# Factorised pair scores with a small tower: 31 units a chunk, TensorE's order written out, later fields transposed in the product ring

## The reference, cut to what matters

```python
e = jnp.stack([tbl_0[ids[:, 0]], ..., tbl_31[ids[:, 31]]], axis=1)      # 512 x 32 x 64
p, q = e[:, ids_x, :], e[:, ids_y, :]                                   # 496 pairs
z = jnp.einsum('bpj,bpj->bp', jnp.einsum('bpi,pij->bpj', p, w), q)      # 512 x 496
h = jnp.concatenate([z, dense_ctx], axis=1)                             # 512 x 512
h = jnp.maximum(h @ W_top1 + b_top1, 0.0)
h = jnp.maximum(h @ W_top2 + b_top2, 0.0)
y = h @ W_top3
```

## Time and profile before

| what | value |
|---|---|
| time, median of 3 runs | 263.83 us (263.15 to 263.94) |
| span of the profiled execution, first to last instruction | 217.7 us |
| around the span (median less span) | 46.1 us |
| PE busy | 196.1 us, 90% |
| DVE busy | 174.1 us, 80% |
| ACT busy | 150.4 us, 69% |
| POOL busy | 150.2 us, 69% |
| mean granted TensorE clock | 0.992 of full speed |

### The profile page before, as it was taken

How to read it: one execution, slowest core, us unless ns; L and a number is a source line. 1 busy time by engine, 2 the same in 40 slices (tenths; PEclk the granted TensorE clock), 3 DMA queues, 4 the chain that set the end, 5 groups by cost and what they waited for, 6 DMA issues and landing times.

```text
span 217.7 us, 6053 instructions
## 1 busy us (share of the span) xinstructions
PE 196.1 (90%) x2072; PEld 131.6 (60%) x2072; DVE 174.1 (80%) x159; ACT 150.4 (69%) x1146; POOL 150.2 (69%) x186
## 2 busy tenths in 40 slices
PE   0029899699999989999999999999999999999985
PEld 0007553575758549556786556865677755767874
DVE  0003789679999999999998999979989989897911
ACT  2010268299799957998199896599959978999201
POOL 4777777777777777777777777777788718777300
PEclk9999999969999999999999999999999999999999
DMA  5666656667111111111111111111110000000000
GB/s 190 252 222 223 230 205 223 218 215 229 30 25 29 35 24 29 29 24 32 25 27 32 27 24 34 25 29 30 29 27 6 2 3 0 2 5 0 3 0 3
DMA packets 6432, 15.21 MB, mean 70 GB/s; under 512 B 2689, under 2 KB 2945, under 8 KB 5250
## 3 DMA queue, kind: packets, MB, share of 16 engines
q1 hardware_dynamic: 2306, 10.62, 13.7%
q0 software_dynamic: 4096, 4.20, 9.3%
HBM read 14.82 MB, written 0.00 MB: 68 GB/s over the span
## 4 chain that ended last, share of the span: by engine, by line
PE 79%; POOL 12%; issue 4%; DMA 3%; ACT 1%; DVE 0%; DVEq 0%
PE pu L485 25%; PE pu L477 24%; PE pz L498 13%; POOL emb L284 12%; PE pt L505 6%; PE pt L452 4%; PE pt L517 3%; DMA emb<-in_tbl,idx 3%; PE pu L505 1%; PE pt L527 1%; DMA idx<-in_ids 1%; PE pt L463 1%; PE pu L517 0%; ACT eT L303 0%; DVE zT L421 0%
## 5 line engine op out<-in xcount | busy, mean ns | idle before, releaser
L284 POOL DMA_INDIRECT emb<-in_tbl,idx x128 | 120.9, 945 | 41.1 <-issue 30.2
L312 ACT ACTIVATE turned<-turned 128x64 f32<-128x64 f32 x544 | 130.2, 245 | 1.5 <-DVE turned L389 1.5
L312 ACT ACTIVATION_READ_ACCUMULATOR turned<-turned 128x1 f32 x544 | 104.1, 191 | 0.0
L389 DVE TENSOR_TENSOR turned<-pu,emb 128x1024 f32<-128x1024 f32 x64 | 75.9, 1215 | 8.1 <-PE pu L477 7.8
L407 DVE TENSOR_TENSOR prod<-pu,eT 128x1024 f32<-128x1024 f32 x48 | 57.1, 1216 | 23.4 <-PE pu L485 23.3
L485 PEld LDWEIGHTS pu<-eT,ws 64*128 64x128 f32 x1024 | 64.9, 198 | 11.8 <-issue 10.4
L485 PE MATMUL pu<-eT,ws 64*128 64x128 f32 x1024 | 69.2, 287 | 0.0
L477 PE MATMUL pu<-ws,eT 64*128 64x512 f32 x256 | 65.5, 612 | 0.0
L303 ACT COPY eT<-pt 128x128 f32<-128x128 f32 (+1 forms) x28 | 11.2, 398 | 41.6 <-PE pt L452 41.6
L270 POOL TENSOR_TENSOR turned<-turned 128x512 f32<-128x512 f32 (+4 forms) x45 | 27.3, 607 | 11.4 <-DVE turned L389 8.4
L477 PEld LDWEIGHTS pu<-ws,eT 64*128 64x128 f32 x256 | 21.1, 186 | 16.7 <-issue 15.1
(11 more groups left out here) (24 smaller groups left out, 25.4 us busy)
## 6 DMA issues: line engine op xcount, KB each, us to landing
ws<-in_w SPq DMA_DIRECT2D x8, 1024.0 KB, 5.0
emb<-in_tbl,idx POOLq DMA_INDIRECT x128, 2.4
w1s<-in_w SPq DMA_DIRECT2D x1, 1024.0 KB
zT<-in_dense SPq DMA_DIRECT2D x1, 512.0 KB, 4.1
w2s<-in_w SPq DMA_DIRECT2D x1, 512.0 KB
idx<-in_ids SPq DMA_DIRECT2D x1, 64.0 KB, 1.8
identity<-in_ident SPq DMA_DIRECT2D x1, 64.0 KB, 1.8
w3s<-in_w SPq DMA_DIRECT2D x1, 1.0 KB
```

What stands on the lines that cost most here:

```text
L284: nc.gpsimd.indirect_dma_start(out=emb[:, c % EC, x, :], out_offset=None, in_=tables[x], in_offset=bass.IndirectOffsetOnAxis(ap=idx[:, c, ...
L312: i = nc.scalar.activation(t, t, ACT.Copy, accum_out=zB[:, b // NT % 2, b % NT * 16 + v:b % NT * 16 + v + 1])
L389: nc.vector.tensor_tensor(turned[:, b % RB, :, :].rearrange("p (x f) i -> p x (f i)", x=2), u.rearrange("p x s i -> p x (s i)"), e, ALU.mu ...
```

## The change

**Units.** 31 units of 16 blocks hold the 496 pairs without empty blocks. The four "b" units are gone; three new units a chunk, "c0" to "c2", hold what they held, each over all 32 fields. "c" units are turned ones (samples on the partitions), but made of eight matmuls of 128 moving columns of weights, since their blocks need different fields as stationary operand. A chunk has 13 "four" units and 3 "c" units turned (16 in all, as before) and 15 units summed (16 before). The dense rows stand in the rows that no pair takes.

**Ring.** The fields of the third and fourth chunk are transposed into buffers of `pu`, eight pairs (a whole buffer) at a time in the third and four in the fourth; such a group takes a turn of the ring, and ACT copies it with one instruction. The first two chunks go through `pt` as before.

**Order.** The order of the units in each chunk, and all of PE's other work (field groups `x`, partition sums `s`, tower steps), is written out in `UNIT_ORDER` and `PLAN`; layer 1 is one step instead of two. `ROWS` is new: ACT sums 38 turned units instead of 34, DVE 16 instead of 21, POOL 10 instead of 9.

**Tail.** In the last chunk each block of layer 1 has its own signal, layer 2 runs over the inputs in the outer loop, and layer 3 takes its two halves as they come.

```diff
     UNITS += [("four", _k, 4 * _m) for _k in range(4 * _j, 4 * _j + 4) for _m in range(_j)]
-    UNITS += [("a", 4 * _j + 3, 4 * _j), ("b", 4 * _j + 3, 4 * _j)]
+    UNITS += [("a", 4 * _j + 3, 4 * _j)]
+UNITS += [(_c, KP - 1, 0) for _c in C_X]
...
+C_X = {"c0": ((0, 3), (5, 3), 1), "c1": ((3, 1), (2, 5), 1), "c2": ((1, 0), (6, 3), 4)}
...
+UNIT_ORDER = [[0, 1, 2, 3, 4, 6, 7, 5, 8, 9, 11, 14, 12, 10, 13, 16, 17, 15, 20, 18, 19, 23, 22, 21, 30, 29, 25, 26,
+               28, 24, 27],
...
-XN = [1, 4, 4, 4]
+X_SIZES = [[1, 1, 1, 1, 1, 1, 1, 1, 1, 1, 1, 1, 1, 1, 1, 1],
+           [4, 4, 4, 4],
+           [8, 8],
+           [4, 4, 4, 4]]
+X_RING = (False, False, True, True)
...
+PLAN = [(-1, 'x', 0), (-1, 'x', 1), (-1, 'x', 2), (-1, 'x', 3), (-1, 'x', 4), (1, 'x', 5), (1, 's', 0), (2, 'x', 6),
+        (2, 's', 1), (3, 'x', 7), (3, 'x', 8), (7, 'x', 9), (7, 'x', 10), (9, 's', 2), (9, 'x', 11), (14, 'x', 12),
...
+            def copy_ring_x(g):
+                c, k, n = GROUPS[g]
+                act.wait_ge(xr_ready, RING_X.index(g) + 1)
+                if c >= EC:
+
+                    act.wait_ge(mult_done, (c - EC + 1) * NU)
+                nc.scalar.copy(eT[:, c % EC, k:k + n, :].rearrange("p s b -> p (s b)"),
+                               pu[:, TURN["x", g] % UR, :, :, :].rearrange("p x s b -> p (x s b)")[:, 0:n * P]).then_inc(xr_read, 1)
...
+            def ring_free(what, v):
+                n = TURN[what, v]
+                if n >= UR:
+                    kind, before = RING[n - UR]
+                    if kind == "u":
+                        pe.wait_ge(mult_done, before + 1)
+                    else:
+                        pe.wait_ge(xr_read, RING_X.index(before) + 1)
+
+            def transpose_ring_x(g):
+                c, k, n = GROUPS[g]
+                ring_free("x", g)
+                for i in range(n):
+                    pe.wait_ge(s_emb[c * KP + k + i], 16 * 2)
+                    mm = nc.tensor.transpose(pu[:, TURN["x", g] % UR, i // 4, i % 4, :],
+                                             emb[:, c % EC, 2 * (k + i):2 * (k + i) + 2, :].rearrange("p f e -> p (f e)"), identity[:])
+                mm.then_inc(xr_ready, 1)
...
+                if UNITS[u][0] in C_X:
+                    for slot in range(4):
+                        for bank in range(2):
+                            x = slot_of(u, bank, slot, 0)[0]
+                            rows = slice(EMB * (x % 2), EMB * (x % 2 + 1))
+                            i = nc.tensor.matmul(pu[:, unit_slot(t), bank, slot, :], eT[rows, c % EC, x // 2, :], ws[rows, u, slot, :],
+                                                 start=True, stop=True)
+                    i.then_inc(u_ready, 1)
+                    return
...
+            for i in L1_LAST:
+                if i < N1 // 2:
+                    pe.wait_ge(h1_act, i + 1)
+                else:
+                    pe.wait_ge(h1_dve, i - N1 // 2 + 1)
+                for n in range(N2):
+                    mm = nc.tensor.matmul(l2_out(last, n), w2s[:, i, n * P:(n + 1) * P], h1[:, i, :],
+                                          start=(i == L1_LAST[0]), stop=(i == L1_LAST[-1]))
```

More of the change, by code:

```diff
@@ L48 @@
 Z_ORDER = [z for z in range(ZCH) if z >= ZA] + list(range(ZA))
-assert NU == 32 and NT == 16 and all(UNITS[u][0] == "four" for u in TURNED)
+assert NU == 31 and NT == 16 and all(UNITS[u][0] != "a" for u in TURNED) and not any(UNITS[u][0] in C_X for u in SUMMED)
 assert ZCH * P == FIELDS * (FIELDS - 1) // 2 + DENSE
-TURN_AT = [TURNED, [5, 6, 7, 8, 9, 14, 16, 17, 18, 19, 20, 21, 22, 23, 26, 29], [2, 6, 7, 8, 9, 10, 14, 16, 17, 22, 23, 24, 26, 27, 28, 30], [0, 5, 9, 10, 11, 13, 14, 15, 18, 19, 20, 22, 23, 24, 25, 26]]
@@ L53 @@
[L53 to L64, removed]
@@ L115 @@
 WU = 4
+NW = -(-NU // WU)
 W_AT_ONCE = 2
-XN = [1, 4, 4, 4]
-GROUPS = [(c, k, XN[c]) for c in range(BCH) for k in range(0, KP, XN[c])]
-NG = len(GROUPS)
[L127 to L134, removed]
@@ new lines, with l1_place @@
+assert [v[0] for v in PLAN] == sorted(v[0] for v in PLAN)
+assert [v[2] for v in PLAN if v[1] == "x"] == list(range(NG))
+SUMS = [v[2] for v in PLAN if v[1] == "s"]
+assert SUMS == list(range(len(SUMS))) and all(v[0] > STEP_A[v[2]] for v in PLAN if v[1] == "s")
+USERS = [v[1:] for v in PLAN if v[1] != "s" and not (v[1] == "x" and in_ring(v[2]))]
+PLACE = {v: i for i, v in enumerate(USERS)}
+def l1_place(c, i):
+    return next(PLACE[part, c] for part in L1_PARTS if i in L1_PARTS[part] and (part, c) in PLACE)
@@ L155, in dlrm_tower, with unit_slot @@
+RING = [v for t in range(-1, NS) for v in [("u", t)] * (t >= 0) + [v for v in TURNS[t] if v[0] == "x" and in_ring(v[1])]]
+TURN = {v: n for n, v in enumerate(RING)}
+NR = len(RING)
+PT_X = [g for what, g in USERS if what == "x"]
+RING_X = [g for what, g in RING if what == "x"]
+assert all(v[0] == "u" for v in RING[NR - UR:])
+def unit_slot(t):
+    return TURN["u", t] % UR
+Z_OUT = [33, 65, 92]
 def dlrm_tower(nc, tables, ids, w, dense, w1, b1, w2, b2, w3, ident, out):
@@ L219, in cols, with x_copied @@
             return slice(c * P, (c + 1) * P)
-        def by_vector(c, n, of):
-            return c == last and n >= of // 2
+        def x_copied(engine, c, k):
+            if not X_RING[c]:
+                engine.wait_ge(pt_read, PLACE["x", GROUP_OF[c, k]] + 1)
+            else:
+                engine.wait_ge(xr_read, RING_X.index(GROUP_OF[c, k]) + 1)
+        L1_LAST = (0, 2, 1, 3)
         def l1_out(c, n):
@@ L325, in layer1 @@
                     act.wait_ge(h2_ready, c)
-                for n in range(2 * half, 2 * half + 2):
-                    i = nc.scalar.activation(h1[:, n, :], l1_out(c, n), ACT.Relu, bias=b1s[:, n:n + 1])
+                for n in ns:
+                    i = nc.scalar.activation(h1[:, n, :], pt[:, n, :], ACT.Relu, bias=b1s[:, n:n + 1])
                 i.then_inc(pt_read, 1)
```

299 lines of the change are left out of this document (165 added, 134 removed), and 11 rows, old and new, of the table PLAN.

## The result

| | time, us (median; lowest to highest) |
|---|---|
| kernel before | 263.88 (263.15 to 264.08) |
| changed kernel | 267.90 (266.14 to 268.95) |
| ratio, 95% interval | 1.016 (1.013 to 1.019) |

What follows compares the result with a forecast made beforehand. PE was taken to bound the kernel from some 42 us to z3. z3 3.6 us sooner, +0.7 +0.5 +0.5 for waits, seams and ring, -0.3 tail: -2.2, so 215.5 plus 46.1 around it is 261.6 us; range 259.7 to 264.4.

Steps and rivals of the forecast that it cites:

- The 46.1 us around it, taken as unchanged.: Time outside the profiled execution, added to the forecast 215.5 us to give 261.6 us.
- x19 starts sooner: Second chunk's last field group on PE: forecast to start at 84.2 us, against 87.77 in the profile before.
- the tail is shorter: After z3, starting the first half of the last chunk's final steps one matmul sooner saves 0.3 us (0 to 0.5).
- PE is there before 84.05 and waits for the last field.: At x19, PE arrives by 81.9 or 83.6 us, before the second chunk's last gather lands at 84.05.
- x19 later than 85 us: Sign of being wrong: the first chunk would cost more than the prediction thought.
- 117.6 + 0.7 + 0.5 + 0.5 - 0.3: From x19 to z3: PE work 117.6, layer 2 wait 0.7, seams 0.5, ring 0.5, transposes before the wait -0.3 us.
- A "c" unit at 0.89: PE's price in us for a new eight-matmul unit, taken from a summed unit; 1.78 if matmuls don't overlap.
- the copy of 1024 columns at 1.0 us: ACT's copy of a ring buffer's field group, 128x1024: 1.0 us by slope, 0.58 as lower end.
- The seams of "c1" and "c2", taken as 0.5: Nine seams after x19 where two same-half matmuls meet: 0 to 0.11 us each; the skill's rule says full 0.11.
- The rivals: All cover holds, 259.9 us (0.18); clock falls, 263.3 (0.13); ACT bounds, 264.8 (0.13); slow "c" units, 269.6 (0.03).
- The slower side: Rival: ACT becomes the bound between x19's copy and the copies behind step 92, giving 264.8 us; chance 0.13.
- the clock fall behind x19: Rival: PE waits 2 us at x18 or x19 and its clock drops, +1.7 us, 263.3 us; chance 0.13.

Runs made afterwards that it cites:

- e1: The kernel before, unchanged, run and profiled once more: 260.5 us.
- e2: The changed kernel, unchanged, run and profiled once more: 266.5 us, ratio 1.024 to the kernel before.
- e7: Changed kernel with early first-chunk row sums b = 0 and 2 moved from ACT to DVE, b = 3 and 4 to later steps: ratio 1.012 to the kernel before.
- e11: Kernel before with 32 gathers instead of 128: only fields 0 to 7 of each chunk gathered, the others filled once by plain transfers: 218.6 us.
- e12: Changed kernel with 32 gathers instead of 128, other fields filled once by plain transfers: 219.5 us.
- e13: Changed kernel with 32 gathers and early first-chunk row sums b = 0 and 2 moved from ACT to DVE, b = 3 and 4 later: 217.2 us.
- e4: Changed kernel with only the first 1 MB of the 8 MB of unit weights loaded, every unit reading one of four blocks: 271.5 us.
- e3: Kernel before with only the first 1 MB of the 8 MB of unit weights loaded, every unit reading one of four blocks: 264.3 us.
- e17: Kernel before without gathers: SP brings every field's rows by 128 plain transfers with the same semaphore counts: 214.0 us.

## Why the prediction was wrong, step by step

*"The 46.1 us around it, taken as unchanged."* Wrong, and the root. They lie inside the span of the timed executions: 216.7 with 32 gathers, 256.3 with 128. Had I asked why a span of 217.7 stands beside a time of 263.8, the profile would have been known as one of another kind.

The sum had three terms against the kernel before: x19 starts sooner, the work from x19 to z3 is longer, the tail is shorter. From TensorE's timelines, us:

| | x19 starts | x19 to z3 | z3 to the end |
|---|---|---|---|
| before, profile ahead of the prediction | 87.7 | 117.3 | 12.6 |
| changed, forecast | 84.2 | 119.0 | 12.3 |
| before, timed (e1) | 116.5 | 127.1 | 12.6 |
| changed, timed (e2) | 118.4 | 133.8 | 12.0 |
| changed, rows to DVE (e7) | 115.6 | 135.0 | 12.0 |
| before, 32 gathers (e11) | 85.4 | 118.7 | 12.6 |
| changed, 32 gathers (e12) | 85.4 | 120.3 | 12.0 |

In the timed executions x19 came 1.9 us later instead of 3.6 sooner, and the stretch behind it grew by 6.6 us instead of 1.7. Both steps failed, about equally.

*"PE is there before 84.05 and waits for the last field."* This is the first step of the sum that failed. The first chunk's loss was costed at nothing because x19 would wait for its gather anyway. In the timed executions the 64th gather is issued at 94.2 us (e1) and 100.2 (e2), and PE comes to x19 only at 116.5 and 118.4. The rows are GpSimd's 64th gather and TensorE's x19 and z3, of e1 and then of e2:

```profile
94.15 0.94 POOL L284 DMA_INDIRECT emb<-in_tbl,idx  x1 [0.30 <-issue]
...
116.51 0.66 PE L452 MATMUL pt<-identity,emb 128*128 128x128 f32 x4
...
243.64 0.44 PE L463 MATMUL pt<-identity,zB 128*128 128x128 f32 x2
```
```profile
100.21 0.94 POOL L340 DMA_INDIRECT emb<-in_tbl,idx  x1 [0.30 <-issue]
...
118.37 0.65 PE L544 MATMUL pt<-identity,emb 128*128 128x128 f32 x4
...
252.13 0.44 PE L555 MATMUL pt<-identity,zB 128*128 128x128 f32 x2
```

Landing takes 2.4 us, so no wait for a gather stood there to hide anything, and the sign of being wrong, x19 later than 85 us, came. What made PE late is in part ACT's row sums ahead of x9's copy, which I had seen, but not counted: without them x19 comes 2.8 us sooner (e7 against e2) and, with fast hand-offs, 2.3 (83.1 in e13 against 85.4). With fast hand-offs the term is 0.0 and not -3.6: e11 and e12 both start x19 at 85.4, where I had PE ready at 83.6.

*PE's work from x19 to z3 and the waits in it.* 117.6 + 0.7 + 0.5 + 0.5 - 0.3 was forecast, about 1.7 more than before. With fast hand-offs it is 1.6 more: right in total, though not in its parts. Within it PE waited 0.4 us for ACT at layer 2 (0.7 forecast) and 1.8 once for DVE, which the sum didn't have. In the timed executions it is 6.6 more (e2 against e1), and this is the second step that failed: PE is idle for 7.8 us against 4.1, mostly for DVE's multiplications, and its groups take 126.0 against 123.1. VectorE's waits from x19 to z3, of e1, e2 and e12 (us in total, times, longest):

```profile
DVE turned L389 <- PE pu L477: 7.4, 9, 1.6
DVE prod L407 <- PE pu L485: 6.8, 7, 1.7
```
```profile
DVE prod L483 <- PE pu L584: 8.2, 7, 2.2
DVE turned L474 <- PE pu L569: 7.2, 2, 6.6
...
DVE prod L483 <- PE pu L576: 5.1, 5, 1.6
```
```profile
DVE turned L483 <- PE pu L578: 7.2, 2, 6.6
```

The longest, 6.6 us, stands at step 67, where sums, layer 1, x21 and layer 2 follow one another on PE and no unit is ready for DVE. But it stands in e12 as well, where the stretch is only 1.6 us longer: it belongs to the order and is not what slow hand-offs add. That a whole field group in a ring buffer leaves fewer units to cover a slow hand-off is my reading of the third chunk (+3.2 us timed, +0.1 with 32 gathers); no run undid the ring alone, so which part of the new order costs these us stays open.

*Sizes.* A "c" unit at 0.89 was right (chain of the changed kernel: start us, us), and so was the copy of 1024 columns at 1.0 us; the tail's 0.3 was 0.6 (12.6 against 12.0):

```profile
137.93 0.89 PE pu L569 x16
```
```profile
L367 ACT COPY eT<-pu 128x1024 f32<-128x1024 f32 x2 | 2.0, 1020 | 0.6 <-PE pu L535 0.6
```

The seams of "c1" and "c2", taken as 0.5, cost nothing. From the last matmul of one unit to the first of the next, start to start, e12's trace has 0.105 us at seven of the nine seams, as between two summed units, and 0.42 at the two behind a turned unit, as between a turned and a summed one. So the trace doesn't agree with the rule by which each would cost 0.11. In e12's chain "c0" and "c1" take 0.20 + 2 x 0.89, and two summed units behind "c1" 1.79:

```profile
92.62 1.99 PE pu L578 x32
94.61 1.79 PE pu L593 x32
```

*The rivals.* None came. The slower side was argued with ACT behind x19; there PE waited for ACT for only 0.5 us (e2), and ACT was late before it. (The 264.8 had no sum behind it: +2.1 on 261.6 is 263.7, no slower than before.) Nor did the clock fall behind x19: from x19 to z3 it was granted at 1.00 in e1 and e2. It did fall in the stalls, but there it weighs little: two executions of e4 at mean clocks of 0.930 and 0.994 took 272.0 and 271.0 us. Whether the forecast would hold in an execution like the one profiled, with 128 gathers and fast hand-offs, stays open, since no run was one; with x19 at e12's 85.4 the gain there would be about 2.3 us and not 3.6, by my estimate.

## What to carry to other kernels

Before a sum is made on a trace, set its span beside the time of the executions that are timed; where tens of us lie between, find them first. A loss may be costed at nothing only if the wait that hides it is there in those executions. Where gathers by POOL slow every hand-off, their number is the lever: moving them or pausing between them gave back 0.6% at best, and here the order written for close hand-offs between PE, ACT and DVE lost more by them: 1.0 us behind the old one with 32 gathers, 6.0 with 128.

## What the runs showed of the hardware

- While POOL issued gathers, hand-offs from PE to DVE took up to 12.4 us before 50 us and mostly 1 to 2.4 us in the chunks after that (e1), and 0.05 us from 194 us on, where the gathers run out; in the profile ahead of the prediction it was 0.05 us throughout. Single pauses of an engine grew to 31.5 us (e3). 128 transfers by SP, in a queue of 20,738 packets, cost nothing of the kind (214.0 us, e17).
- The trace loses records of gathers: of the 2,048 semaphore counts of their landings it holds 686 in e1, against all 2,048 of the transfers in e17 and 2,026 in the profile ahead of the prediction. The Trainium skill, "NOTIFIC — the notification-queue block", section "7.1 Overflow: three behaviours, one of which stalls the engine", says that the block which writes such records does one of three things when a queue is full, by its setting: it discards the new record, overwrites old ones, or stalls the producer. A stalled producer would fit the pauses, but no run here shows the setting or can switch the recording off, and e12 lost 224 of 512 counts while 21 of 23 waits of DVE's multiplications still ended 0.05 us after PE: argued, not shown.
- Why one execution of the kernel before (span 217.7) had all gathers and none of the stalls stays open.
